# Leaving out waits that an engine has already made

## The reference, cut to what matters

```python
# layer 0: causal attention of 16 heads of 16; cross attention to a context; a dequantised feed-forward with LoRA
# layer 1: attention of 16 heads of 128 over eight sequences; cross attention of 8 heads, without weights
# then 64 experts, 8 of them for each token:
probs = softmax(x @ gate_w.T);  weights, chosen = top_k(probs, 8);  weights /= weights.sum()
y = sum(weights[k] * (w2[e] @ (silu(w1[e] @ x) * (w3[e] @ x))) for k, e in enumerate(chosen))
```

## Time and profile before

| | |
|---|---|
| median of three runs | 811.34 us (808.4 to 811.78) |
| the profiled execution: its time, its span | 814.26 us, 812.9 us |
| mean granted TensorE clock | 0.976 |
| instructions in the span | 17140 |
| busy: TensorE matmuls, weight loads | 736.4 us (91%), 607.9 us (75%) |
| busy: VectorE, ScalarE, GpSimd | 496.7 us (61%), 369.5 us (45%), 371.7 us (46%) |
| moved by DMA | 132.00 MB, 162 GB/s |

### The profile page before, as it was taken

The page is one execution under the profiler, slowest core; times in us unless marked ns, Lnnn a source line. Parts: engine busy times, 40 slices in busy tenths (PEclk is TensorE's granted clock), DMA queues, the critical chain, the costliest instruction groups (busy, mean ns, idle before and its releaser), DMA issues.

```text
span 812.9 us, 17140 instructions
## 1 busy us (share of the span) xinstructions
PE 736.4 (91%) x5723; PEld 607.9 (75%) x5723; DVE 496.7 (61%) x1520; ACT 369.5 (45%) x962; POOL 371.7 (46%) x488
## 2 busy tenths in 40 slices
PE   8999999999999999999999777749988899888975
PEld 6667877878787888888777554338887787888854
DVE  4887878666657665877688665425454445434335
ACT  3465546443555566667776333412222222344325
POOL 1142221233734444435687544563555555555535
PEclk9999999999999999999999998959999999999998
DMA  9465430011356554333464389247768898633266
GB/s 241 108 213 180 136 109 8 1 40 44 102 131 204 173 172 137 111 112 87 150 172 123 86 310 344 83 135 262 226 196 269 270 291 291 197 116 96 82 235 251
DMA packets 95598, 132.00 MB, mean 162 GB/s; under 512 B 29511, under 2 KB 65905, under 8 KB 95256
## 3 DMA queue, kind: packets, MB, share of 16 engines
q1 hardware_dynamic: 86344, 113.57, 45.8%
q0 software_dynamic: 9168, 17.35, 5.8%
HBM read 116.29 MB, written 35.58 MB: 187 GB/s over the span
## 4 chain that ended last, share of the span: by engine, by line
PE 64%; DVE 7%; issue 6%; another core or an unknown queue 6%; DMA 6%; POOL 4%; ACT 4%; SPq 3%; DVEq 0%; POOLq 0%; ACTq 0%
PE ps L214 58%; PE ps L217 6%; DMA rows_e<-x_slots 1%; POOL x_slots L1639 1%; SPq L1261 1%; ACT soft L585 1%; DMA rowso<-y_slots 1%; DMA y_slots<-o_e,index_e 1%; DMA wh<-in_wqkv 1%; POOL w_lo L1131 1%; ACT pTc L1477 1%; DVE topc L1527 1%; DMA w_sb<-in_w 1%; POOL y_slots L2034 1%
## 5 line engine op out<-in xcount | busy, mean ns | idle before, releaser
L2034 POOL DMA_INDIRECT y_slots<-o_e,index_e x127 | 124.4, 980 | 111.8 <-DVE o_e L2025 72.6
L1131 POOL TENSOR_TENSOR w_lo<-wh,w_hi 128x256 fp32r<-128x256 f32 x120 | 91.6, 771 | 101.6 <-ACT w_hi L1005 100.0
L214 PE MATMUL ps<-xT_e,w_slot 128*128 128x128 f32 x760 | 99.2, 280 | 7.4 <-issue 7.0
L2015 DVE TENSOR_TENSOR h_e<-ps,gate_e 128x256 f32<-128x256 f32 x64 | 26.9, 421 | 120.2 <-ACT gate_e L1962 91.3
L214 PEld LDWEIGHTS ps<-xT_e,w_slot 128*128 128x128 f32 x760 | 92.0, 195 | 10.6 <-issue 9.9
L1639 POOL DMA_INDIRECT x_slots<-rows_all,index_all x64 | 62.7, 979 | 23.9 <-issue 17.7
L1956 ACT COPY xT_e<-ps 128x512 f32<-128x512 f32 x64 | 37.1, 580 | 72.8 <-PE ps L217 28.5
L214 PE MATMUL ps<-x_hi,w_hi 128*128 128x512 f32 (+1 forms) x240 | 69.9, 372 | 0.1
L1962 ACT ACTIVATE gate_e<-ps 128x256 f32<-128x256 f32 x64 | 24.6, 384 | 96.7 <-PE ps L214 49.0
L1005 ACT CAST w_hi<-wh 128x256 fp32r<-128x256 f32 x120 | 47.8, 407 | 41.2 <-PE ps L214 37.5
L214 PE MATMUL ps<-x_lo,w_hi 128*128 128x512 f32 (+1 forms) x240 | 64.1, 349 | 0.0
(11 more groups left out here) (288 smaller groups left out, 1734.6 us busy)
## 6 DMA issues: line engine op xcount, KB each, us to landing
w_slot<-in_we SPq DMA_DIRECT2D x95, 384.0 KB
rows_e<-x_slots SPq DMA_DIRECT2D x127, 136.0 KB
wh<-in_wqkv SPq DMA_DIRECT2D x40, 384.0 KB, 3.2
x_slots<-blank SPq DMA_DIRECT2D x4, 2176.0 KB, 9.5
w_kept<-in_we SPq DMA_DIRECT2D x20, 384.0 KB
sums<-key_sums SPq DMA_DIRECT2D x24, 256.0 KB
wo<-in_wo SPq DMA_DIRECT2D x40, 128.0 KB
rowso<-y_slots SPq DMA_DIRECT2D x10, 512.0 KB, 7.6
```

What stands on the lines that cost most here:

```text
L214: return self.pe.matmul(out, lhsT, rhs, start=start, stop=stop, skip_group_check=shared)
L1131: pool.tensor_tensor(t.w_lo[n % 2][:, :, which, :], t.wh[n % 2][:, :, which, :], t.w_hi[n % 2][:, :, which, :], ALU.subtract).then_inc(*t. ...
L2015: dve.tensor_tensor(T.h[:, 0:n, :].rearrange("p s t -> p (s t)"), ExpertBanks(m, p - 1).up[:, 2 * P:(2 + n) * P], T.gate[:, 0:n, :].rearra ...
L2034: pool.indirect_dma_start(m.y_slots, bass.IndirectOffsetOnAxis(ap=T.index[:, s:s + 1], axis=0), T.o[:, s, :], None, bounds_check=TOK * TOP ...
```

## The change

A small object for each of TensorE, VectorE and ScalarE remembers the highest count that its engine has waited for on each semaphore. A wait for that count or a lower one is not written into the program; any other is written as before. All the waits of these three engines go through it, `Banks.take` included. The waits of SyncE and GpSimd stay as they are.

```diff
+class Waits:
+    def __init__(self, engine):
+        self.engine, self.made = engine, {}
+
+    def __call__(self, sem, value):
+        if self.made.get(sem.num, -1) < value:
+            self.made[sem.num] = value
+            self.engine.wait_ge(sem, value)
...
         self.pe, self.act, self.dve, self.pool, self.sp = nc.tensor, nc.scalar, nc.vector, nc.gpsimd, nc.sync
+        self.pe_wait, self.act_wait, self.dve_wait = Waits(self.pe), Waits(self.act), Waits(self.dve)
...
-    def take(self, pe, *use):
+    def take(self, wait, *use):
...
         for sem, value in latest.values():
-            pe.wait_ge(sem, value)
+            wait(sem, value)
...
     def turn(p):
...
         if p >= 2:
-            pe.wait_ge(*t.rowsT(p - 1))
+            m.pe_wait(*t.rowsT(p - 1))
         for s, j in enumerate(tiles_of(p)):
-            pe.wait_ge(*t.rows_in[j % WORK](j // WORK + 1))
+            m.pe_wait(*t.rows_in[j % WORK](j // WORK + 1))
...
     def up(p):
...
-        pe.wait_ge(*t.rowsT(p + 1))
+        m.pe_wait(*t.rowsT(p + 1))
         if p >= 3:
-            pe.wait_ge(*t.h(p - 2))
+            m.pe_wait(*t.h(p - 2))
...
-            pe.wait_ge(*t.w_ready[j])
+            m.pe_wait(*t.w_ready[j])
...
-                act.wait_ge(*t.up_ps(p - PAIRED + 1))
+                m.act_wait(*t.up_ps(p - PAIRED + 1))
...
-                dve.wait_ge(*t.down_ps(p - PAIRED))
+                m.dve_wait(*t.down_ps(p - PAIRED))
...
     def add(n, b):
         place = BY_PE[b][n]
-        pe.wait_ge(*t.diag_set(n * NSEQ + b + 1))
-        pe.wait_ge(*t.there(place, b))
+        m.pe_wait(*t.diag_set(n * NSEQ + b + 1))
+        m.pe_wait(*t.there(place, b))
```

More of the change, by code:

```diff
@@ L413, in weights @@
             if r:
-                pe.wait_ge(*t.weights(r))
+                m.pe_wait(*t.weights(r))
             for o in range(0, 1024, width):
@@ L537, in sequence @@
         yield
-        pe.wait_ge(*t.x2T(b + 1))
+        m.pe_wait(*t.x2T(b + 1))
         if b == 0:
-            pe.wait_ge(*t.weights(2))
+            m.pe_wait(*t.weights(2))
         for j, bank in enumerate((q, p)):
@@ L548, in sequence @@
         for j, done in enumerate((t.up_act, t.up_dve)):
-            pe.wait_ge(*done(b + 1))
+            m.pe_wait(*done(b + 1))
             if b == 0:
-                pe.wait_ge(*t.weights(4))
+                m.pe_wait(*t.weights(4))
             for mo in range(4 * j, 4 * j + 4):
@@ L937, in projections @@
             if n in (0, H1):
-                pe.wait_ge(*t.x_lo_set(n // H1 + 1))
+                m.pe_wait(*t.x_lo_set(n // H1 + 1))
             for which in range(3):
-                pe.wait_ge(*t.w_lo_set(3 * n + which + 1))
-                bank = banks.take(pe, "qkv"[which], n)
+                m.pe_wait(*t.w_lo_set(3 * n + which + 1))
+                bank = banks.take(m.pe_wait, "qkv"[which], n)
                 w_hi, w_lo = t.w_hi[n % 2], t.w_lo[n % 2]
@@ L1363, in turn_tops @@
         def turn_tops():
-            pe.wait_ge(*t.top_set(4 * b + 4))
-            banks.take(pe, "tops", b)
+            m.pe_wait(*t.top_set(4 * b + 4))
+            banks.take(m.pe_wait, "tops", b)
             pair = banks.pair("tops", b)
@@ L1399, in sequence @@
         if b == 0:
-            pe.wait_ge(*t.gate_in(1))
-            mean = banks.take(pe, "mean")
+            m.pe_wait(*t.gate_in(1))
+            mean = banks.take(m.pe_wait, "mean")
             for k in range(KD):
@@ L1417, in sequence @@
         yield
-        pe.wait_ge(*t.avs_set(b + 1))
-        columns = banks.take(pe, "columns", b)
+        m.pe_wait(*t.avs_set(b + 1))
+        columns = banks.take(m.pe_wait, "columns", b)
         for x in range(2 * KD):
@@ L1446, in fills @@
         for k in count():
-            bank = banks.take(pe, "fill", k)
+            bank = banks.take(m.pe_wait, "fill", k)
             for _ in range(2):
@@ L2169, in dve_combine @@
     dve, chain = m.dve, m.dve_chain
-    dve.wait_ge(*te.weight(NSEQ * TOPK + 1))
+    m.dve_wait(*te.weight(NSEQ * TOPK + 1))
     def begin(b):
         place = BY_DVE[b]
-        dve.wait_ge(*t.there(place, b))
+        m.dve_wait(*t.there(place, b))
         dve.scalar_tensor_tensor(out=t.part[:, b, :], in0=t.rows[:, b, place, :], scalar=r.weight_all[:, b, place:place + 1],
@@ L2200, in act_diagonal @@
     if n == 0:
-        m.act.wait_ge(*te.weight(NSEQ * TOPK + 1))
-        m.act.wait_ge(*te.down_ps(max(ORDER.index(e) for e in range(LAST_KEPT, KEPT)) // 2 + 1))
+        m.act_wait(*te.weight(NSEQ * TOPK + 1))
+        m.act_wait(*te.down_ps(max(ORDER.index(e) for e in range(LAST_KEPT, KEPT)) // 2 + 1))
     m.act.activation(t.diag[k][:, b, :], m.ident[:, :], ACT.Copy, scale=r.weight_all[:, b, BY_PE[b][k]:BY_PE[b][k] + 1]).then_inc(*t.diag_set.one)
```

442 lines of the change are left out of this document (221 added, 221 removed).

## The result

The changed kernel takes 805.76 us (median of 19 runs, 794.14 to 812.18), the kernel before 812.2 in the same comparison (19 runs, 803.04 to 819.25). The ratio is 0.9893, 95% interval 0.9862 to 0.9923. It leaves out the runs that are more than 1.5% above the fastest of their kernel, though the clock granted in these is hardly lower (0.962 to 0.975 in the changed kernel, 0.965 to 0.978 in its other runs); the means of all 19 runs give 0.9899. Forecast were 810.0 us, with a range from 806.0 to 813.0. The kernel got faster by 1.1% where 0.16% was forecast.

A forecast was written before the change was run, and what follows sets the result against it. TensorE's matmuls, busy 736.4 of 812.9 us, were taken as the bound. Gains of 1.05 us on TensorE and 0.3 on VectorE, summed as 1.3 us or 0.16%, took the 811.34 us median to 810.0, range 806.0 to 813.0.

The forecast's parts named there:

- The counts: Whole kernel: 226 wait instructions go on TensorE, 224 on ScalarE, 139 on VectorE, 589 of 17140, busy counts unchanged.
- What lies beside other work: All three engines: most removed waits are hidden behind other work; of at most 18.3 us, 1.3 us is gained.
- 202 of TensorE's 226: TensorE's removed wait instructions that start over 0.1 us ahead of their weight load: claimed to cost nothing.
- the expert rounds take 232 us as before: Expert rounds, 545 to 777 us: length unchanged, the array's busy time the same within 1 us per stretch.
- issue waits that 51 ns don't make: TensorE matmuls' own issue waits: 13.8 and 7.2 us in 24 pieces, most near 1 us, too long for one wait instruction.
- nothing to be had: Rival, TensorE's 24 waits without lead: even these are hidden; gain 0, 811.3 us, chance 0.33.
- The queue that the sequencer fills ahead of its engine: All three engines: instructions queue, 64 deep on TensorE, 8 on VectorE and ScalarE, while the sequencer reads on; the 202 cost nothing.
- The stretch from 376 to 529 us: On the chain: fifteen TensorE waits without lead at 0.07 us each, 1.05 us, so about 1 us shorter.
- the pace rival: TensorE's stream: handing over instructions binds the array, so every removed wait gains; 5.8 to 11.5 us, chance 0.12.
- The sign: Expert rounds, 545 to 777 us: shortening by 3 us or more would show that the sequencer's pace did bind.
- Instruction fetch: Rival, TensorE in the expert rounds: moved piece boundaries cause four waits of 1.5 us; 4.7 us slower, 816.0 us, chance 0.06.
- The chance of 0.11 for faster: Whole kernel: probability given to a measured time below 807.3 us; same had 0.84, slower 0.05.

The follow-up runs named there:

- e18: Kernel before, all waits made, with two GpSimd fills of 8 columns after each second scatter of the expert rounds: 794.47 us, ratio 0.9784 to before.
- e2: Changed kernel with every wait made again in the expert rounds, redundant ones left out everywhere else: 821.8 us, ratio 1.0021 to the kernel before.
- e9: Kernel before with two redundant waits of the expert rounds, one on ScalarE and one on VectorE, made five times: 820.91 us, ratio 0.9982.
- e13: Kernel before with every scatter of the expert rounds replaced by a plain store of as many rows in order: 789.44 us, ratio 0.9638.
- e15: The changed kernel as it is, measured again in another comparison: 817.83 us against 818.43 for the kernel before, ratio 1.0004.
- e3b: Kernel before with one GpSimd fill of 256 columns after each second scatter of the expert rounds: 814.06 us, ratio 1.0023.

## Why the prediction was wrong

**The counts held.** 589 instructions fewer, engine by engine as worked out, with the busy counts as they were.

**The step that failed is "What lies beside other work".** There I set 202 of TensorE's 226 and nearly all of the other two engines' waits to zero, and took the stage's length as given: "the expert rounds take 232 us as before". TensorE was busy 209.07 of these 232 us, and I called the rest issue waits that 51 ns don't make. That is so, but those 23 us then need a cause of their own, and the sum has no term for it. Most of them were the long rounds of the pattern of three, and these go with GpSimd's unbroken runs of scatters: with the same scatters spaced out (e18) the late hand-overs fall from 107 to 9 us and the rounds from 225.9 to 201.6. Whether a round is long is not fixed by the instructions in it, so an edit that costs and saves nothing of its own can still move the stage. The profiled pair differs by 14.3 us there, and the kernels of the table span 195.5 to 231.9.

**What the waits themselves cost.** With the slow rhythm taken away in two ways the change is worth -0.4% and +0.1%, each to about 0.7%: too coarse to tell the forecast 0.16% from none. e2 is finer and speaks for the rival of nothing to be had. In e9 the 244 satisfied waits more would take 122 x 17 + 122 x 21 ns = 4.6 us, 0.6%, if all were on the path; its interval ends at 1.0020. The queue that the sequencer fills ahead of its engine, weighed in the prediction from the Trainium skill (Advanced Engine Details and Errata, Sequencer and Instruction Queues), agrees with that: what failed was not this rule but the belief that nothing else moves.

The same belief failed outside the rounds. The stretch from 376 to 529 us was to be about 1 us shorter, because "each step that starts 0.07 us sooner pulls its consumers along". From ScalarE's fourth activation that writes pTc to its eighth copy to avsc (375.9 to 526.2 us in the kernel before) it is 150.3 us before and 156.8 after. Over all profiles it is 150.3 to 154.9 us in the seven kernels with all waits and 150.1 to 157.4 in the eight without the redundant ones there, so no gain of 1 us shows. One piece of it in the kernel before and two in the changed one:

```profile
412.41 0.60 PE L217 MATMUL ps<-ident,topc 128*128 128x128 f32 x4
```

```profile
414.85 0.43 DVE L1125 TENSOR_TENSOR vT<-vT,sums 128x256 f32<-128x256 f32 x1 [2.42 <-DMA sums<-key_sums]
...
416.47 0.66 PE L230 MATMUL ps<-ident,topc 128*128 128x128 f32 x4 [2.21 <-DVE topc L1540]
```

TensorE now waits 2.21 us for VectorE's topc, which is late because VectorE stood 2.42 us ahead of it for a load. Why the load is late here is open.

**The rivals.** Of the pace rival the sign came true, rounds shorter by 3 us or more, and the cause did not: TensorE alone gives 0.3%, where all of the gain was asked of it. The sign was badly chosen, since anything that shortens the rounds makes it. Instruction fetch did not show. The pieces are 46 in place of 47, and the issue waits that it was to lengthen fell. They go with the slow rhythm: at the products with loaded weights, in the kernel before, the changed one and e13, which has 47 pieces too, they are 7.0 us, 3.5 us and none:

```profile
L214 PE MATMUL ps<-xT_e,w_slot 128*128 128x128 f32 x760 | 99.2, 280 | 7.4 <-issue 7.0
```

```profile
L227 PE MATMUL ps<-xT_e,w_slot 128*128 128x128 f32 x760 | 98.5, 281 | 3.6 <-issue 3.5
```

```profile
L214 PE MATMUL ps<-xT_e,w_slot 128*128 128x128 f32 x760 | 95.9, 278 | 0.0
```

**The range.** The measured 805.76 lies 0.24 us below it. The chance of 0.11 for faster was that of one rival; a stage with a rhythm of its own should have had chances on both sides.

**What stays open.** Two things. The first is by what the change shifts the rhythm. Of the nine kernels that leave out waits of the rounds and keep the scatters as they are, eight measure from 0.9890 to 0.9970 and one, e15, 1.0004; the three that keep all waits of the rounds (e2, e3b, e9) lie from 0.9982 to 1.0023. So the sign is hardly an accident of one comparison, but which wait does it, and why e15 has nothing of it, can't be told from the runs. The chip needn't be the reason: that of e15 had medians of 813.63 and 818.43 us for the kernel before in two comparisons. The second is by which way a run of scatters holds up TensorE's hand-overs. That it does is shown by e18, which differs from the kernel before in the fills alone, and by e13. The Trainium skill (Perfetto Trace Analysis, Tensor Engine Instruction) says that the end of a matmul in the profile is an estimate, and that PSUM's acknowledgement and the spread of the semaphore come after it. The trace agrees in that 3.6 us can lie between that end and the reader's start, but doesn't tell which of the two is late.

## What to carry to other kernels

Before pricing an edit in a loop over a few buffers, look at the spacing of its rounds. If it repeats in groups, as 3.09, 3.09 and 4.8 us here, the idle time in it can be a rhythm that an edit shifts, and a gain of 1% measured there may be such a shift and no work saved. Take the rhythm away (here 0.6 us more between the scatters of two rounds) and measure the edit again.

## What the hardware showed that was not expected

Runs of GpSimd scatters without a break hold up what TensorE hands to ScalarE and VectorE: in the kernel before 0.04 us in the median under the first scatter of a run, 2.06 under the fourth, up to 3.8. Plain stores of as many packets don't (6 us in 192 hand-overs, 107 before). A spacing of 1.89 us in place of 1.28 between the scatters of two rounds was enough, 1.48 was not. The kernel before has medians from 812.2 to 820.07 us in the seven comparisons here, two of them (813.63 and 818.43) on the same chip, so a difference of 1% between runs of different comparisons says nothing.
